# Query/key root norms by Newton steps on GpSimd, fp32 products in strips of 32 columns, and a new table of steps

## What is computed

```
x  = x + attn0(LN(x)) + ffn0(LN(x))       # layer 0
x  = x + attn1(LN(x)) + ffn1(LN(x))       # layer 1

attn0: q_c = rms_norm(x W) * w_q ; k_c = rms_norm(x W') * w_k ; k_c and q_c get a further part from x
       rms_norm(y) = y * rsqrt(mean(y*y over the 8 channels of a head) + 1.19e-7) * w
       scores = q k / sqrt(8), causal, softmax, times values, times W_O
ffn0:  sigmoid(xr W_r) * (relu(xk W_k)^2 W_v), xr and xk mixed of x and the token before
attn1: scores with a bias by position, softmax, values, projection with a bias
ffn1:  gelu(x W1) W2, W1 and W2 composed of 32 weighted low-rank products
```

## Time and profile before

| | |
|---|---|
| runs | 1700.98, 1699.41, 1707.15 us, median 1700.98 |
| span of the profiled execution | 1697.2 us, 3.8 us under the median |
| instructions | 33267 |
| busy: TensorE, VectorE, ScalarE, GpSimd | 1499.7, 1378.8, 1290.5, 935.7 us |
| the costliest group | 1664 exps (L961) of 600 ns, 909.0 us |
| chain that ended last | TensorE 53%, ScalarE 16%, VectorE 14%, GpSimd 8% |

### The profile page before, as it was taken

One profiled execution on the slowest core, in us unless ns is written; L12 is line 12 of the kernel. 1 busy time (PEld: TensorE's weight loads), 2 busy tenths in 40 slices (PEclk: granted clock), 3 DMA queues, 4 the chain that ended last, 5 costly groups with the idle time before them and its releaser, 6 DMA issues.

```text
span 1697.2 us, 33267 instructions
## 1 busy us (share of the span) xinstructions
PE 1499.7 (88%) x11850; PEld 624.7 (37%) x11850; DVE 1378.8 (81%) x2538; ACT 1290.5 (76%) x2550; POOL 935.7 (55%) x1176
## 2 busy tenths in 40 slices
PE   4778888888888888888899999999999999999995
PEld 2644444444444444433233323233333323332331
DVE  2378888888888888888888898888888888889880
ACT  2258878878878787766788788888888888888884
POOL 2135555555555555554655655566556656565565
PEclk9879999999999999999999999999999999999998
DMA  8332332232222223322321223123321233122300
GB/s 289 63 57 76 76 73 76 76 73 79 76 75 74 78 64 74 81 63 49 79 70 51 57 53 68 57 51 57 64 66 51 48 64 74 51 58 48 67 15 19
DMA packets 133125, 116.41 MB, mean 69 GB/s; under 512 B 16856, under 2 KB 125664, under 8 KB 132960
## 3 DMA queue, kind: packets, MB, share of 16 engines
q1 hardware_dynamic: 126272, 100.64, 25.3%
q0 software_dynamic: 4096, 8.40, 1.5%
q10 hardware_dynamic: 2592, 5.24, 0.9%
HBM read 79.63 MB, written 33.55 MB: 67 GB/s over the span
## 4 chain that ended last, share of the span: by engine, by line
PE 53%; ACT 16%; DVE 14%; POOL 8%; issue 5%; DMA 3%; SPq 1%; DVEq 0%; POOLq 0%; ACTq 0%
PE pv_acc L639 16%; PE scores_transposed L655 13%; ACT probs L961 7%; PE scores_transposed L793 4%; PE scores_transposed L765 4%; PE scores_for_max L676 4%; DVE maxs L1171 3%; POOL x_between_layers L1259 2%; PE scores_for_max L801 2%; PE scores_for_max L705 2%; DVE maxs L1174 2%; POOL probs L1315 1%; DVE maxs L1202 1%; ACT xn L862 1%; POOL parts L1242 1%
## 5 line engine op out<-in xcount | busy, mean ns | idle before, releaser
L961 ACT ACTIVATE probs<-scores_transposed 128x512 f32<-128x512 f32 x1664 | 909.0, 600 | 178.3 <-PE scores_transposed L655 170.5
L655 PE MATMUL scores_transposed<-stacks 62*128 62x512 bf16 (+3 forms) x2048 | 583.5, 346 | 50.5 <-ACT probs L961 34.8
L639 PE MATMUL pv_acc<-probs,vals 128*32 128x512 f32 (+3 forms) x4096 | 469.3, 530 | 49.3 <-POOL probs L1315 25.4
L1341 POOL TENSOR_TENSOR probs<-probs,near_bias 128x512 f32<-128x512 f32 x256 | 329.6, 1290 | 327.0 <-ACT probs L961 326.1
L1171 DVE TENSOR_REDUCE maxs<-scores_for_max 128x2 f32<-128x1024 f32 x325 | 390.7, 1221 | 77.0 <-PE scores_for_max L676 76.3
L655 PEld LDWEIGHTS scores_transposed<-stacks 62*128 62x128 bf16 x2048 | 155.5, 94 | 603.8 <-ACT probs L961 304.0
L676 PE MATMUL scores_for_max<-stacks 60*128 60x512 bf16 x1024 | 328.7, 384 | 11.4 <-DVE maxs L1171 9.1
L1174 DVE TENSOR_REDUCE maxs<-scores_for_max 128x1 f32<-128x512 f32 x374 | 245.9, 684 | 16.1 <-PE scores_for_max L676 12.0
L680 PE MATMUL scores_for_max<-stacks 60*128 60x512 bf16 (+3 forms) x1024 | 248.9, 312 | 10.9 <-DVE maxs L1199 6.1
L1202 DVE TENSOR_REDUCE maxs<-scores_for_max 128x1 f32<-128x512 f32 x256 | 175.4, 685 | 82.4 <-PE scores_for_max L692 80.0
L1315 POOL TENSOR_SCALAR_AFFINE_SELECT probs<-probs 128x512 f32<-128x512 f32 x256 | 159.6, 638 | 76.7 <-ACT probs L961 76.4
(11 more groups left out here) (131 smaller groups left out, 1982.8 us busy)
## 6 DMA issues: line engine op xcount, KB each, us to landing
stacks<-parts_scratch SPq DMA_DIRECT2D x768, 64.0 KB
parts_scratch<-parts SPq DMA_DIRECT2D x64, 384.0 KB, 2.6
x_tile<-in_L_attn_x_dram SPq DMA_DIRECT2D x16, 256.0 KB, 2.8
probs<-in_fc_B_dram ACTq DMA_DIRECT2D x1, 4096.0 KB, 19.5
stage_a<-in_fc_A_T_dram SPq DMA_DIRECT2D x1, 4096.0 KB, 16.8
stacks<-mT SPq DMA_DIRECT2D x256, 4.0 KB
x_res<-in_L_attn_x_dram SPq DMA_DIRECT2D x16, 256.0 KB, 3.3
x_tile<-x_between_layers SPq DMA_DIRECT2D x16, 256.0 KB
```

The costliest lines, as they stand in the source:

```text
L639: last = mm(acc[VW * j:VW * j + VW, q0:T], columns[:, first:first + VW], probs[:, row, column:column + width], start=(kt == 0 and pu % PAI ...
L655: last = mm(st[:, bank, column:column + T - q0], ks[p][rows, h, P * kt:P * kt + P], qs[p][rows, h, q0:T], start=True, stop=True)
L961: fn(probs[:, row, :], st[:, B.use(("st", u, number)).bank, :], ACT.Exp, scale=SCALE).then_inc(s["exp_done"], 1)
L1341: g.tensor_tensor(diag, diag, near_bias[:, kt, :].unsqueeze(1).broadcast_to([P, G, P]), ALU.mult).then_inc(s["emul_pool"], 1)
```

## The change

The root. VectorE no longer takes a reciprocal: it makes ssq = -(mean + eps)/2 and, from the bits of it as an integer, a first guess of the inverse root. GpSimd then makes three Newton steps of four dependent operations on 128x128 elements, at slots 38, 40 and 42. ScalarE has no ROOT. The scaling waits for all twelve.

The strips. A fp32 product with 128 stationary columns becomes four with 32 columns each, into four strips of 32 partitions of the same bank: FR, FK, FV, H0 to H3, PR, VP, Y0 to Y3, and QT and KT of layer 1. The transposes and PJ0, PJ1 stay as they are.

The table. Slots move, and five pieces of work that hung on another entry get entries of their own.

```diff
 WORK_USES = {
-    0: {"MT0": (1, 0, 0), "FR": (4, 0, 1), "FK": (8, 0, 1), "OA": (17, 0, -1), "MT1": (23, 0, 0),
-        "XT": (24, 0, 2), "PJ0": (27, 0, 2), "PJ1": (30, 0, 2), "MT2": (35, 0, 0), "FV": (43, 0, 1),
+    0: {"MT0": (1, 0, 0), "FR": (4, 0, 1), "FK": (5, 0, 1), "OA": (15, 0, -1), "MT1": (22, 0, 0),
+        "XT": (24, 0, 2), "PJ0": (27, 0, 2), "PJ1": (30, 0, 2), "MT2": (33, 0, 0), "FV": (46, 0, 1),
         "OB": (49, 0, 0), "QT": (50, 0, 2), "MT3": (51, 0, 1), "KT": (54, 1, 2)},
-    1: {"H0": (1, 0, 1), ...   "VP": (31, 0, 1), ...
+    1: {"H0": (2, 0, 1), ...   "VP": (33, 0, 1), ...
 OTHER_WORK = {
     0: {...
-        "STORE": (25, -1), "SQUARE": (32, 2), "MEAN": (36, 2), "ROOT": (42, 2), "SCALE_QK": (43, 2)},
-    1: {"LN": (0, 2), "NORM": (17, 2), "BESIDE": (23, -1), "STORE": (39, -1)},
+        "STORE": (25, -1), "SQUARE": (32, 2), "MEAN": (36, 2), "ROOT": (38, 2), "SCALE_QK": (45, 2),
+        "POW": (8, 2), "SECOND_Q": (51, 2), "THIRD_Q": (52, 2), "SECOND_K": (54, 2), "THIRD_K": (57, 2),
+        "KACT": (9, 1), "SCALE_K": (47, 2)},
+    1: {"LN": (0, 2), "NORM": (16, 2), "BESIDE": (23, -1), "STORE": (39, -1), "POW": (1, 2),
+        "SECOND_Q": (36, 2), "THIRD_Q": (39, 2), "SECOND_K": (46, 2), "THIRD_K": (47, 2)},
...
+            def mm_strips(out, columns, moving, **group):
+                for c in range(0, P, STRIP):
+                    last = mm(out[c:c + STRIP], columns[:, c:c + STRIP], moving, **group)
+                return last
...
-                                last = mm(work[:, P * t:P * t + P], fa[:, P * t:P * t + P], wrkv[:, 0, :],
-                                          start=True, stop=True)
+                                last = mm_strips(work[:, P * t:P * t + P], fa[:, P * t:P * t + P], wrkv[:, 0, :],
+                                                 start=True, stop=True)
...
-                            link(v.tensor_scalar(ssq[:], ssq[:], 1.0 / HD, RMS_EPS, ALU.mult, ALU.add),
+                            link(v.tensor_scalar(ssq[:], ssq[:], -0.5 / HD, -0.5 * RMS_EPS, ALU.mult, ALU.add),
                                  "rms", 4, 2, 2)
-                            v.reciprocal(ssq[:], ssq[:]).then_inc(s["rms"], 1)
+                            v.tensor_scalar(rrms[:].bitcast(I32), ssq[:].bitcast(I32), -0.5, ROOT_GUESS, ALU.mult,
+                                            ALU.add).then_inc(s["rms"], 1)
...
+                def root_turn(n):
+                    steps = ((turn, rrms, rrms, ALU.mult), (turn, turn, ssq, ALU.mult),
+                             (turn, turn, three_halves, ALU.add), (rrms, rrms, turn, ALU.mult))
+                    if n == 0:
+                        pool.wait_ge(s["rms"], B.count(4, 3, 2))
+                    for i, (to, one, other_, op) in enumerate(steps):
+                        if n or i:
+                            pool.wait_ge(s["root_done"], B.count(4 * ROOT_TURNS, 4 * n + i, 2))
+                        g.tensor_tensor(to[:], one[:], other_[:], op).then_inc(s["root_done"], 1)
...
+                        for n in range(ROOT_TURNS):
+                            if B.after("ROOT", slot, 2 * n):
+                                root_turn(n)
```

More of the change, by code:

```diff
@@ L38 @@
 GELU_C, GELU_K = 0.7978845608028654, 0.044715
+ROOT_GUESS = float(0x5F3759DF - 2 ** 22 - 2 ** 30)
+ROOT_TURNS = 3
 Q_PARTS = (0, 0, 1, 0, 1, 2)
@@ L372, in build @@
         half = sb("minus_half", [P, NT * 32])
+        three_halves = sb("three_halves", [P, NT * 32])
+        turn = sb("turn", [P, NT * 32])
         ident = sb("ident", [P, P])
@@ L728, in other @@
                             pe.wait_ge(s["mix_done"], B.count(3, 3, 1))
-                            mm(work, wrkv[:, 1, :], fb[:], start=True, stop=True).then_inc(full, 1)
+                            mm_strips(work, wrkv[:, 1, :], fb[:], start=True, stop=True).then_inc(full, 1)
                         if B.due("FV", slot):
@@ L733, in other @@
                             for t in range(NT):
-                                last = mm(work[:, P * t:P * t + P], fd[:, P * t:P * t + P], wrkv[:, 2, :],
-                                          start=True, stop=True)
+                                last = mm_strips(work[:, P * t:P * t + P], fd[:, P * t:P * t + P], wrkv[:, 2, :],
+                                                 start=True, stop=True)
                             last.then_inc(full, 1)
@@ L764, in other @@
                                 work = claim(f"H{f}")
-                                mm(work, w1[:, P * f:P * f + P], xnT[:, B.parity(1), 1:T + 1],
-                                   start=True, stop=True).then_inc(full, 1)
+                                mm_strips(work, w1[:, P * f:P * f + P], xnT[:, B.parity(1), 1:T + 1],
+                                          start=True, stop=True).then_inc(full, 1)
                         if B.due("AT", slot):
@@ L776, in other @@
                             for t in range(NT):
-                                last = mm(work[:, P * t:P * t + P], attT[:, P * t:P * t + P], wproj[:],
-                                          start=True, stop=True)
+                                last = mm_strips(work[:, P * t:P * t + P], attT[:, P * t:P * t + P], wproj[:],
+                                                 start=True, stop=True)
                             last.then_inc(full, 1)
@@ L782, in other @@
                             for t in range(NT):
-                                last = mm(work[:, P * t:P * t + P],
-                                          xnT[:, B.parity(1), 1 + P * t:1 + P * t + P], wqkv[:, 2 * P:3 * P],
-                                          start=True, stop=True)
+                                last = mm_strips(work[:, P * t:P * t + P],
+                                                 xnT[:, B.parity(1), 1 + P * t:1 + P * t + P], wqkv[:, 2 * P:3 * P],
+                                                 start=True, stop=True)
                             last.then_inc(full, 1)
@@ L792, in other @@
                                 for f in range(NF):
-                                    last = mm(work[:, 0:D], big[:, f, P * t:P * t + P], w2[:, f, :],
-                                              start=(f == 0), stop=(f == NF - 1))
+                                    last = mm_strips(work[:, 0:D], big[:, f, P * t:P * t + P], w2[:, f, :],
+                                                     start=(f == 0), stop=(f == NF - 1))
                                 last.then_inc(full, 1)
@@ L800, in other @@
                                     taken_out("XT")
-                                mm(work, wqkv[:, P * side:P * side + P], xnT[:, B.parity(2), 1:T + 1],
-                                   start=True, stop=True).then_inc(full, 1)
+                                mm_strips(work, wqkv[:, P * side:P * side + P], xnT[:, B.parity(2), 1:T + 1],
+                                          start=True, stop=True).then_inc(full, 1)
                 for u in range(NG):
@@ L869, in other @@
                             first_part(side)
-                        if B.out(name, slot, 1):
+                        if B.due("SECOND_" + name[0], slot):
                             second_part(side)
@@ L894, in other @@
                             fn(sqr[:], big[:, :, 0:2 * P], ACT.Square).then_inc(s["sq_done"], 1)
-                        if B.due("ROOT", slot):
-                            act.wait_ge(s["rms"], B.count(4, 3, 2))
-                            fn(rrms[:], ssq[:], ACT.Sqrt).then_inc(s["root_done"], 1)
                     else:
@@ L1267, in other @@
                             store_rows(t)
-                    if B.after("LN", slot, 1):
+                    if B.due("POW", slot):
                         pool.wait_ge(s["ln"], B.count(3, 3, 2))
@@ L1273, in other @@
                     if layer == 0:
-                        if B.out("FK", slot, 1):
+                        if B.due("KACT", slot):
                             pool.wait_ge(s["act_taken"], B.use("FK").taken[1])
@@ L1284, in other @@
                                             ).then_inc(s["post"], 1)
-                        if B.after("SCALE_QK", slot, 1):
+                        for n in range(ROOT_TURNS):
+                            if B.after("ROOT", slot, 2 * n):
+                                root_turn(n)
+                        if B.due("SCALE_K", slot):
                             pool.wait_ge(s["rms"], B.count(4, 4, 2))
@@ L1301, in other @@
                     for side, name in enumerate(("QT", "KT")):
-                        if B.out(name, slot, 2):
+                        if B.due("THIRD_" + name[0], slot):
                             third_part(side)
```

14 lines of the change are left out of this document (8 added, 6 removed), and 4 rows, old and new, of the table WORK_USES.

## The result

The changed kernel takes **1745.2 us** (median, 1740.2 to 1761.3) where the kernel before takes 1700.2 us on the same chip: ratio **1.0265, 95% interval 1.0222 to 1.0309**. The forecast was 1716 us, range 1665 to 1742: 29 us too short. The profiled execution has 1761.3 us for its span of 1759.6 us; it is the slowest of its four, so its bodies are read beside those of after_again.

A forecast was written before the change was run, and what follows sets the result against it. Second layer bound by TensorE's work, first layer by its waits. First-layer bodies +2.5 - 1.1 + 0.5 - 0.1 = +1.8 us, fifteen +27 us; second layer -12; together +15 us, median 1716 us, range 1665 to 1742.

The forecast's parts named there:

- The root, +2.5 us a body: First-layer bodies: GpSimd's Newton turns delay slot 48's mask and the scaling, so TensorE reaches slot 52 2.5 us later.
- the first rival: First layer: freed ScalarE shortens slot 48's wait and the half-clocked stretches behind it; 1652 or 1676 us, chance 0.33.
- the third: First-layer rival: MT2 costs 1.4 us and longer waits halve the clock, 0.7 us a body more; 1740 us, chance 0.13.
- The scaling at 1.22 us: VectorE's scaling of the norms in a first-layer body, on the path to slot 52, taken as 1.22 us.
- With their gaps: On the path to slot 52: scaling 1.22, two products 2.6, split 0.5, mask 0.65 us, gaps between them included.
- The table, -1.1 + 0.5: First-layer bodies: moved slots win two waits of 0.54 us, 1.1 us at most; MT2 two slots sooner costs 0.5.
- MT2's 0.5: First-layer bodies: MT2 at slot 33 instead of 35 lengthens TensorE's wait for the split maxima; 0.5 us, bounds 0 to 1.4.
- The strips, second layer -12 us: Second layer, where TensorE is the bound: products in strips save 0.8 us a body, 12 us over sixteen bodies.
- the last rival: Strips bound by instruction issue: a set takes 1.8 us, not 1.16; about 1790 us, chance 0.04.
- the first layer's -0.1 us: First-layer bodies: strips of FR, FK and FV save 0.2 us, counted as 0.1 because FV's part falls into the wait.
- The released ScalarE wins: First rival: if a GpSimd operation takes 0.25 us or less, freed ScalarE wins; 1652 or 1676 us, chance 0.33.
- The table hurts and the clock falls: Third rival, first layer: MT2 costs 1.4 us and longer waits halve the clock; 1740 us, chance 0.13.

The follow-up runs named there:

- after_again: The changed kernel itself measured once more on another chip: ratio 1.0355 to the kernel before.
- root_fill: The kernel before with the Newton root on GpSimd alone, plus 18 matmuls without a use ahead of slot 48's product: ratio 1.0262 to the kernel before.
- root_only: The kernel before with the Newton root on GpSimd alone, old table and full products: ratio 1.0414 to the kernel before.
- strips_table: The changed kernel with the root back on ScalarE at slot 42, so strips and new table alone: ratio 0.9896 to the kernel before.
- strips_table_2: The changed kernel with the root back on ScalarE at slot 42, repeated in another job: ratio 0.9991 to the kernel before.
- table_only: The kernel before with the new table alone, root on ScalarE and full products: ratio 0.9976 to the kernel before.
- after: The changed kernel as first measured, with root, strips and table: 1745.2 us, ratio 1.0265 to the kernel before.
- jobs 1 and 2: Two of five measuring jobs, each on its own chip with its own executions of the kernel before; the changed kernel had 1.0265 in job 1.
- strips_only: The kernel before with the fp32 products in strips alone, root on ScalarE and old table: ratio 1.0008 to the kernel before.
- one_turn: The changed kernel with one Newton step on GpSimd in place of three: ratio 0.9971 to the kernel before.
- root_only_2: The kernel before with the Newton root on GpSimd alone, repeated in another job: ratio 1.0332 to the kernel before.
- root_mask_first_2: The kernel before with the root on GpSimd alone, its third turn moved behind slot 48's mask, scaling and key products later: ratio 1.0351.

## Why the prediction was wrong

**The root, +2.5 us a body: this is the step that failed, and what it left out is the clock.** Each of its rows came true: 0.40 and 0.45 us (taken: 0.40 and 0.46), the mask of slot 48 behind the turns, the scaling waiting for GpSimd. root_fill, with the clock kept up, puts the queue's share at 2.1 us, and at slot 52, where the forecast had +2.5, at 2.3 (15.6 - 13.3). What the sum lacked stood in the earlier trace rows: behind a wait TensorE's clock is at its lower level. The forecast knew this, but used it only to credit a shorter wait in the first rival and 0.7 us in the third; its own term made the wait before slot 48 longer and kept the clock as it was, that is, put the time behind the wait at nothing more. The runs show 2.05 us a body there. Measured, the root costs 3.3 to 4.1% (root_only twice; the changed kernel over strips_table 3.7%, over strips_table_2 3.6%), 57 to 70 us or 3.8 to 4.7 us in each of 15 bodies, in place of 37.

**The scaling at 1.22 us: too short.** It takes 1.58 us as a mean, 1.63 in the fourteen bodies where GpSimd's mask runs beside it, and its 0.36 us lie on the path to slot 52; they are part of the 2.1. "With their gaps" covered this in part.

**The table, -1.1 + 0.5:** the net of -0.6 stands against -0.5 in table_only's profile; 0.5 is less than a pair of profiles resolves, and its ratio of 0.9976 doesn't exclude nothing. MT2's 0.5 was neither shown nor refuted.

**The strips, second layer -12 us:** near in the profile of after, 0.58 us x 16 = 9 us, and in jobs 1 and 2. A set of 32 matmuls took 1.08 us: the last rival fell. By the 62 ns for each MATMUL with hardware decoding off, which the Trainium skill gives (TensorE: Matmul & The Clock Gate, Wait — 56ns, not 53.3ns?), a set is estimated at 2.0 us; no run here shows that. On three other chips a new wait takes the gain away. And strips_only, with its 1.0008, doesn't show the gain in the time: whether the first layer's -0.1 us was wrong by some 0.9, as its profile has it, stays open.

**The rivals.** "The released ScalarE wins" fell by its own condition, 0.45 us against 0.25, and one_turn shows that ScalarE's loads weren't worth anything even with a short chain. "The table hurts and the clock falls" named 1740 us, close to the result, with half of the cause: the clock did fall, but for the root's wait and not for MT2's. The sum made afterwards, from the profiles: root 2.1 and clock 2.05, less 0.5 for the table, is 3.65 us a body, 55 us; less 9 us for the second layer it is 46 us, and 45 were measured. That it comes so close is in part chance: the two profiles of the changed kernel have 4.61 and 3.21 us more a body than the kernel before (47.90 and 46.50 less 43.29), and in the second the 9 us are missing.

## What to carry to other kernels

Before work is moved to an engine that is "only 55% busy", look at what stands behind it in that engine's queue within the next few slots, and add its length to the wait of whoever needs that. When a wait of TensorE grows, price it twice: once for itself, and once for the stretch behind it at half clock, which cost as much again here. Before the change the wait at slot 48 was 1.3 to 1.9 us, and behind it the clock fell in four bodies of thirteen; with the root alone it was 3.3 to 3.5 us, and the clock fell in all of 25. Independent work in the gap took the second price back in root_fill; where the wait was shorter it gained nothing that can be told; and a gain under 1% needs the same comparison on more than one chip.

## What was not expected of the hardware

A wait of 3.5 us was followed by some 9 us at a granted clock of 0.50 in 20 of 25 bodies (root_only and root_only_2), one of 2.2 us (after) or three of 1.4 us (root_mask_first_2) by some 6 us in most of thirteen; 18 matmuls without a use in the gap kept it at 1.00 in all thirteen. A two-operand operation of VectorE on 1024 elements took 1.63 us with 0.55 us of GpSimd's mask beside it and 1.22 us without. And one and the same code had, on some chips, a copy on ScalarE that started 0.84 us late in every second-layer body (0.91 less 0.07), on others never.
